# Third layer's time mixing (L2x): new x summed in the PSUM, copied out by ScalarE with sums and squares of the rows; VectorE's statistics for the last element only

## The reference, cut to what matters

```
x = x + tanh(g_xattn[2]) * wkv(time_decay, time_first, k=layernorm(x), v=ctx)
# wkv, per element and channel, w = -exp(time_decay), u = time_first:
#   y_t  = (e^(u+k_t) v_t + p_t) / (e^(u+k_t) + q_t)
#   p_t+1 = e^w p_t + e^(k_t) v_t ,  q_t+1 = e^w q_t + e^(k_t)      (computed with a running maximum)
x = x + tanh(g_ffn[2]) * experts(layernorm(x))       # needs mean and variance of each row of the new x
```

## Time and profile before

| | us |
|---|---|
| median of 3 runs (1809.58 to 1811.84) | 1811.55 |
| the profiled execution | 1814.82 |
| its span | 1813.1 |
| first and last VectorE instruction of L2x | 741.48 to 877.03 |

### The profile page before, as it was taken

One profiled execution on the slowest core, in us unless ns is written; L12 is line 12 of the kernel. 1 busy time (PEld: TensorE's weight loads), 2 busy tenths in 40 slices (PEclk: granted clock), 3 DMA queues, 4 the chain that ended last, 5 costly groups with the idle time before them and its releaser, 6 DMA issues. The chain is left out here.

```text
span 1813.1 us, 23758 instructions
## 1 busy us (share of the span) xinstructions
PE 1345.1 (74%) x6498; PEld 1003.8 (55%) x6518; DVE 1464.4 (81%) x3194; ACT 884.1 (49%) x1742; POOL 546.7 (30%) x560
## 2 busy tenths in 40 slices
PE   4799228886999677244662597179999899998788
PEld 2454114443788443243520486168888788877676
DVE  5999378984877568799579699796999889988785
ACT  3454356662333262353420242138888788843343
POOL 0000004543110021200004023303777577766552
PEclk8999759997999856566785799599999999999999
DMA  5010420000000120254100010405788799888874
GB/s 174 23 36 1 191 76 1 0 0 1 1 1 1 48 95 1 89 189 151 47 30 11 24 41 6 122 0 163 240 241 254 203 274 261 247 261 245 226 235 156
DMA packets 92284, 197.91 MB, mean 109 GB/s; under 512 B 16040, under 2 KB 25384, under 8 KB 91312
## 3 DMA queue, kind: packets, MB, share of 16 engines
q0 software_dynamic: 27120, 91.25, 18.0%
q1 hardware_dynamic: 65088, 105.82, 17.8%
HBM read 181.30 MB, written 15.73 MB: 109 GB/s over the span
## 5 line engine op out<-in xcount | busy, mean ns | idle before, releaser
L2246 POOL DMA_INDIRECT L3f_gd<-rows,idx x160 | 189.8, 1186 | 200.7 <-DVE L3f_gd L2475 176.1
L2246 POOL DMA_INDIRECT L3f_gu<-in_L_ffn_e_up,idx x160 | 168.9, 1056 | 71.3 <-issue 47.2
L2314 PE MATMUL L3f_o_ps<-L3f_euh,L3f_ath 128*128 128x512 f32 x352 | 146.0, 415 | 21.0 <-DVE L3f_atl L2456 20.9
L2302 PE MATMUL L3f_h_ps<-L3f_xh,L3f_edh 128*128 128x512 f32 (+1 forms) x384 | 145.1, 378 | 8.2 <-DVE L3f_xl L2461 8.2
L926 POOL TENSOR_TENSOR L0f_hq<-L0f_hid,magic 128x1408 bf16<-128x1408 f32 x16 | 45.2, 2826 | 338.9 <-DVE L0f_hid L997 338.9
L2302 PE MATMUL L3f_h_ps<-L3f_xh,L3f_edl 128*128 128x512 f32 (+1 forms) x384 | 144.5, 376 | 0.0
L2302 PE MATMUL L3f_h_ps<-L3f_xl,L3f_edh 128*128 128x512 f32 (+1 forms) x384 | 144.5, 376 | 0.0
L2286 PE MATMUL L3f_g_ps<-L3f_oh 128*128 128x128 f32 x704 | 97.6, 283 | 61.9 <-DVE L3f_oh L2443 61.9
L2314 PE MATMUL L3f_o_ps<-L3f_eul,L3f_ath 128*128 128x512 f32 x352 | 138.2, 393 | 0.0
L2314 PE MATMUL L3f_o_ps<-L3f_euh,L3f_atl 128*128 128x512 f32 x352 | 138.0, 392 | 0.0
L2286 PEld LDWEIGHTS L3f_g_ps<-L3f_oh 128*128 128x128 f32 x704 | 91.4, 195 | 72.5 <-issue 68.0
(11 more groups left out here) (529 smaller groups left out, 3669.5 us busy)
## 6 DMA issues: line engine op xcount, KB each, us to landing
L3f_eu<-in_L_ffn_e_up SPq DMA_DIRECT2D x96, 256.0 KB, 4.6
L3f_ed<-in_L_ffn_e_down SPq DMA_DIRECT2D x96, 256.0 KB, 4.4
L2x_ed<-in_L_ffn_e_down SPq DMA_DIRECT2D x32, 256.0 KB, 3.4
rows<-L2x_eo SPq DMA_DIRECT2D x32, 256.0 KB, 2.4
ternary_wgu<-in_L_ffn_w_gate_upT SPq DMA_DIRECT2D x4, 1408.0 KB, 10.3
X<-in_x SPq DMA_DIRECT2D x4, 1024.0 KB, 10.6
L0x_V<-in_ctxT SPq DMA_DIRECT2D x8, 512.0 KB, 3.4
L1f_C<-in_ctx SPq DMA_DIRECT2D x2, 2048.0 KB, 13.1
```

Of the source, the lines that this page charges most:

```text
L2246: pool.indirect_dma_start(buf[j % ND][:, :], None, table, bass.IndirectOffsetOnAxis(ap=idx[:, j:j + 1], axis=0)).then_inc(sem[j % ND], 16)
L2302: last = pe.matmul(h_ps[h][:, 0:cols], lhsT=w[h][:, c, :], rhs=x[:, c, 0:cols], start=(c == 0 and m == 0), stop=(c == DC - 1 and m == 2))
L2314: last = pe.matmul(o_ps[a][:, :], lhsT=w[h][:, a * P:(a + 1) * P], rhs=x[h][:, :], start=False, stop=False)
```

## The change

It applies to L2x alone (`own` is `not first`).

- `turn_back(b)`: the eight transposes become matmuls of y against `turner` (the identity times minus the tanh of the gate), added to what the PSUM holds. `begin_x(b)` puts X there first, by one f32 matmul 128x512 against the identity for each tile; it stands in TensorE's turn i behind the first two `turn_rows` and waits for the x of batch i-1 (`x_ready`).
- `add_to_x` is gone from VectorE. ScalarE's `keep_x(b)` copies the sum from the PSUM to X, with the sum of each row (`accum_out`), in turn b+1 between the first two `keep_rows` and `invert`. For the last element it copies without sums, and VectorE runs `bn_stats` on its two tiles.
- GpSimd makes the mean of each row from the sum (`mean_ready`); ScalarE's `deviate(b)` squares the distance to the mean, with its sum, at the end of turn b+1; the statistics of the next stage are filled in the form in which `bn_stats` leaves them (two equal halves' means, one sum of squares, one zero).
- VectorE computes `den` between the scans of q and p; before, it stood behind both.
- `turner` (128x128) is made by VectorE in place of `ntg` (128x1), ahead of the first statistics.

```diff
--- before.py
+++ after.py
@@ -167,6 +170,14 @@
     xn_ready, turned, ek_ready, ev_ready, q_ready, p_ready = (ph.sem(n) for n in ("xn", "turned", "ek", "ev", "q", "p"))
     den_ready, s_ready, p0_ready, ln_ready, r_ready = (ph.sem(n) for n in ("den", "s", "p0", "ln", "r"))
     t_ready, m_ready, y_ready, yT_ready, x_ready = (ph.sem(n) for n in ("t", "mr", "y", "yT", "x"))
+    own = not first
+    if own:
+        rowsum, part = ph.sb("rowsum", [P, NT]), ph.sb("part", [P, 1])
+        dev = [ph.sb(f"dev{j}", [P, D], BF16) for j in range(TB)]
+        part_made, mean_ready, dev_ready = ph.sem("part"), ph.sem("mean"), ph.sem("dev")
+    if not first:
+        turner = ph.sb("turner", [P, P])
+        turner_made = ph.sem("turner")
     if first:
         g = ph.sb("g", [P, 8])
         W, LT, tio = ph.sb("W", [P, DC, 2 * D]), ph.sb("LT", [P, DC, T]), ph.sb("tio", [P, T])
@@ -269,11 +280,22 @@
         def turn_back(b):
             pe.wait_ge(y_ready, b + 1)
             for j in range(TB):
+                if b and first:
+                    pe.wait_ge(x_ready, TB * (b - 1) + j + 1)
+                for c in range(DC):
+                    if first:
+                        last = pe.transpose(y_ps[j][:, c, :], y[:, c, j * P:(j + 1) * P], ident[:, :])
+                    else:
+                        last = pe.matmul(y_ps[j][:, c, :], lhsT=y[:, c, j * P:(j + 1) * P], rhs=turner[:, :],
+                                         start=False, stop=(c == DC - 1))
+                last.then_inc(yT_ready, 1)
+
+        def begin_x(b):
+            for j in range(TB):
                 if b:
                     pe.wait_ge(x_ready, TB * (b - 1) + j + 1)
-                for c in range(DC):
-                    last = pe.transpose(y_ps[j][:, c, :], y[:, c, j * P:(j + 1) * P], ident[:, :])
-                last.then_inc(yT_ready, 1)
+                pe.matmul(y_ps[j][:, :, :].rearrange("p c n -> p (c n)"), lhsT=ident[:, :], rhs=X[:, TB * b + j, :],
+                          start=True, stop=False)
 
         def project_k(b, j):
             if j == 0:
@@ -342,11 +364,16 @@
                 if i:
                     add_up(i - 1, 1)
             else:
+                if not i:
+                    pe.wait_ge(turner_made, 1)
                 if i:
                     turn_back(i - 1)
                 if i + 2 < B:
                     turn(i + 2)
-                for e in range(EU * i, EU * (i + 1)):
+                for e in range(EU * i, EU * i + 2):
+                    turn_rows(e)
+                begin_x(i)
+                for e in range(EU * i + 2, EU * (i + 1)):
                     turn_rows(e)
         if first:
             add_up(B - 1, 0)
@@ -404,6 +431,25 @@
             act.activation(r[:, :, :], den[:, :, :], ACT.Ln).then_inc(ln_ready, 1)
             act.wait_ge(ln_ready, b + 1)
             act.activation(r[:, :, :], r[:, :, :], ACT.Exp, scale=-1.0).then_inc(r_ready, 1)
+
+        def keep_x(b):
+            for j in range(TB):
+                t = TB * b + j
+                act.wait_ge(yT_ready, t + 1)
+                whole = y_ps[j][:, :, :].rearrange("p c n -> p (c n)")
+                if b < B - 1:
+                    act.activation(X[:, t, :], whole, ACT.Copy, accum_out=rowsum[:, t:t + 1]).then_inc(x_ready, 1)
+                else:
+                    act.activation(X[:, t, :], whole, ACT.Copy).then_inc(x_ready, 1)
+
+        def deviate(b):
+            act.wait_ge(mean_ready, b + 1)
+            for j in range(TB):
+                t = TB * b + j
+                if b:
+                    act.wait_ge(dev_ready, t + 1 - TB)
+                act.activation(dev[j][:, :], X[:, t, :], ACT.Square, scale=-1.0, bias=stats[:, t, 1:2],
+                               accum_out=stats[:, t, 2:3]).then_inc(dev_ready, 1)
 
         def keep_rows(e):
             k = e % 2
@@ -469,6 +515,8 @@
             if not first:
                 for e in range(EU * i, EU * i + 2):
                     keep_rows(e)
+                if i:
+                    keep_x(i - 1)
             invert(i)
             if i + 1 < B:
                 first_column(i + 1)
@@ -485,9 +533,15 @@
             else:
                 for e in range(EU * i + 2, EU * (i + 1)):
                     keep_rows(e)
+            if own and i:
+                deviate(i - 1)
         if first:
             for k in range(2):
                 keep(B - 1, k)
+        else:
+            keep_x(B - 1)
+        if own and first:
+            deviate(B - 1)
 
     @block.gpsimd
     def _(pool):
@@ -503,6 +557,14 @@
             for h in range(2):
                 for j in range(2):
                     pool.memset(sv[h][j][:, :, :, HD:HD + 1], 1.0).then_inc(filled, 1)
+        if own:
+            pool.memset(part[:, :], 1.0 / D).then_inc(part_made, 1)
+            pool.wait_ge(part_made, 1)
+            for b in range(B if first else B - 1):
+                pool.wait_ge(x_ready, TB * (b + 1))
+                ts = slice(TB * b, TB * (b + 1))
+                pool.tensor_tensor(stats[:, ts, 1:5:3], rowsum[:, ts].unsqueeze(2).to_broadcast([P, TB, 2]),
+                                   part[:, 0:1].unsqueeze(2).to_broadcast([P, TB, 2]), ALU.mult).then_inc(mean_ready, 1)
 
     @block.vector
     def _(dve):
@@ -526,6 +588,8 @@
             dve.scalar_tensor_tensor(rstd[:, sl], w1[:, sl], 1.5, rstd[:, sl], ALU.add, ALU.mult).then_inc(step, 1)
             dve.wait_ge(step, n + 3)
             dve.scalar_tensor_tensor(nm[:, sl], m[:, sl], -1.0, rstd[:, sl], ALU.mult, ALU.mult).then_inc(nm_ready, 1)
+            if own:
+                dve.memset(stats[:, sl, 5:6], 0.0)
             return n + 3
 
         def make_keys(b):
@@ -557,6 +621,13 @@
                 last = dve.tensor_tensor_scan(q[:, c, 1:T], a[:, c:c + 1].to_broadcast([P, T - 1]), ek[b % 2][:, c, 0:T - 1],
                                               0.0, ALU.mult, ALU.add)
             last.then_inc(q_ready, 1)
+            if not first:
+                dve.wait_ge(q_ready, b + 1)
+                if b:
+                    dve.wait_ge(y_ready, b)
+                for c in range(DC):
+                    last = dve.scalar_tensor_tensor(den[:, c, :], ek[b % 2][:, c, :], eu[:, c:c + 1], q[:, c, :], ALU.mult, ALU.add)
+                last.then_inc(den_ready, 1)
             dve.wait_ge(ev_ready, b + 1)
             if b:
                 dve.wait_ge(s_ready, b)
@@ -567,18 +638,14 @@
 
         def ratio(b):
             h = b % 2
-            dve.wait_ge(q_ready, b + 1)
-            if b:
-                dve.wait_ge(y_ready, b)
             if first:
+                dve.wait_ge(q_ready, b + 1)
+                if b:
+                    dve.wait_ge(y_ready, b)
                 dve.wait_ge(E_ready, b + 1)
                 dve.tensor_tensor(den[:, :, :], E[h][:, :, :], q[:, :, :], ALU.add).then_inc(den_ready, 1)
                 dve.wait_ge(den_ready, b + 1)
                 dve.tensor_tensor(E[h][:, :, :], E[h][:, :, :], V[b % 3][:, :, :], ALU.mult).then_inc(EV_ready, 1)
-            else:
-                for c in range(DC):
-                    last = dve.scalar_tensor_tensor(den[:, c, :], ek[h][:, c, :], eu[:, c:c + 1], q[:, c, :], ALU.mult, ALU.add)
-                last.then_inc(den_ready, 1)
             dve.wait_ge(p_ready, b + 1)
             dve.wait_ge(p0_ready, b + 1)
             if b:
@@ -645,8 +712,8 @@
             dve.wait_ge(made, 1)
             dve.tensor_scalar(kb[:, :], kb[:, :], -1.0, 19.0, ALU.mult, ALU.add).then_inc(u_ready, 1)
             dve.tensor_scalar(u[:, :], u[:, :], 83.0, None, ALU.min).then_inc(u_ready, 1)
-            dve.tensor_scalar(ntg[:, 0:1], tg[:, gate:gate + 1], -1.0, None, ALU.mult).then_inc(step, 1)
-            at = row_group(0, 1)
+            dve.tensor_scalar(turner[:, :], ident[:, :], tg[:, gate:gate + 1], -1.0, ALU.mult, ALU.mult).then_inc(turner_made, 1)
+            at = row_group(0, 0)
         if first:
             at = row_group(1, at)
             dve.wait_ge(gated, 1)
@@ -661,7 +728,7 @@
             if first:
                 context(i, 0)
             ratio(i)
-            if i:
+            if first and i:
                 add_to_x(i - 1)
             if first:
                 if 1 < i + 1 < NG:
@@ -670,7 +737,12 @@
             if i + 1 < B:
                 value(i + 1)
             invert(i)
-        add_to_x(B - 1)
+        if first:
+            add_to_x(B - 1)
+        else:
+            for t in range(NT - TB, NT):
+                dve.wait_ge(x_ready, t + 1)
+                dve.bn_stats(stats[:, t, :], X[:, t, :])
 
     ph.end()
 
```

## The result

The changed kernel takes 1801.8 us (median of 7 runs, 1800.05 to 1810.73) against 1811.84 for the kernel before, a ratio of 0.995 with a 95% interval of 0.9933 to 0.9966. The forecast was 1803.0.

What follows compares the result with a forecast made beforehand. VectorE bounds L2x until the squares' ring holds batches 2 to 5. Batch 0 +0.36, batch 1 -1.75, batches 2 to 5 -2.6, batch 6 -1.85, batch 7 -2.15, end -0.6, start +0.1: -8.5, from 1811.55 to 1803.0 us; range 1797 to 1809.

Steps and rivals of the forecast that it cites:

- VectorE is the bound, 2.51 off, 0.65 on: VectorE's batch in L2x: 15.05 us less 2.51 of x and statistics, plus 0.65 of exposed dependences, gives 13.2.
- The two dependences: On VectorE, den directly behind the scan of q and s behind the scan of p: 0.18 us each.
- the third: On VectorE, ev directly behind s: 0.29 us more per batch, already paid in batch 0.
- Copies and squares 1.6 and 1.8: ScalarE's additions per batch: two keep_x copies 1.6 us, two deviate squares 1.8 us, accumulator reads included.
- Batches 2 to 5 at 14.4, held by the squares' ring, -2.6: Ring through turn, keep_rows, row loads, deviate, weigh and normalise sets batches 2 to 5 at 14.4 us, saving 2.6 in all.
- the half microsecond that I granted it: TensorE's clock was expected to rise with begin_x, shortening the squares' ring from 14.9 to 14.4 us.
- The second ring, 13.3, little above VectorE: Ring from turn through keep_x, Ln and Exp, VectorE's L596 to L603 and turn_back: 13.3 us against VectorE's 13.2.
- `turn_back` costs nothing: On TensorE, eight f32 matmuls in place of eight transposes: 1.06 against 1.04 us, so no added time.
- the Trainium skill's rule of four: Rival 4: turn_back's matmuls cost four times the transposes, 6.9 us; second ring 18.5, total 1832 us; chance 0.03.
- Batch 7 -2.15, end -0.6: Last batch, without turn, weigh or normalise, gains 2.15 us; the end behind the last L603 shortens by 0.6.
- the table load: Rival 3: ScalarE's Square needs table loads, 1.28 us each, around each deviate; ring 17.0, total 1816 us; chance 0.07.
- VectorE alone: Rival 1: clock rises enough or rows land sooner, no ring above 13.2 us; total 1798.3 us; chance 0.22.

Runs made afterwards that it cites:

- the half of the change: Changed kernel with new x still copied out of the PSUM by ScalarE, but statistics left to VectorE's bn_stats; ratio 0.9975 to the kernel before, stage 116.29 us.
- the last kernel: Changed kernel with den behind both scans, squares behind normalise, last element's x as before, and zero-weight matmuls added; 1795.68 us against 1810.61 for the kernel before, ratio 0.9916.

## Why the prediction was right, and where it was not

The total was right (8.5 forecast; 8.9 in the stage, 10 in the median), and the bound engine was the right one. That it fits so closely is luck: batches 2 to 5 gave 3.15 us more than forecast, and the last batch and the end 1.34 and 1.80 less, 3.14 together.

- *VectorE is the bound, 2.51 off, 0.65 on* (right): 13.13 us measured against 13.2. The two dependences are 0.14 each in place of 0.18 (the kernel with den early, alone); the third is 0.29 as read from the earlier trace rows, and shows again in the half of the change.
- *Copies and squares 1.6 and 1.8* (too dear): 1.14 and 1.41. The accumulator read does not stand behind the instruction; it starts 0.13 us before its end, and the next starts 0.12 before the read's.
- *Batches 2 to 5 at 14.4, held by the squares' ring, -2.6* (the step that failed): they averaged 13.61 and gave 5.75. The ring is real and of the forecast size where the clock stays low (14.20 to 15.78 without the new matmuls), but the clock rose more than the half microsecond that I granted it: with TensorE at full clock the ring took 12.50 us, from `turn` at 784.65 to the end of `normalise` at 797.15, and bound nothing. Moving the squares out of the ring changed nothing; adding zeros to TensorE removed the waits.
- *The second ring, 13.3, little above VectorE* (the right path, mis-sized): this is the ring that made r late in batches 3 and 5, at 14.07 and 14.12. In batch 3 `turn_back` took 3.57 of it and not 1.7; the other four terms, 4.0, 1.6, 2.2 and 3.8, measured 3.41, 1.14, 2.19 and 3.76. With `turn_back` at full clock, in the kernel with zeros, it was no longer above VectorE's 13.13.
- *`turn_back` costs nothing* (wrong): it doubled, 2.05 us against 1.04 at full clock. The error is in reading: eight entries of L304 are four matmuls of the code, since each f32 matmul shows as two instructions, while a transpose is one. begin_x was mis-sized in the same way: 1.98 us at full clock, not 0.9. So TensorE got about 2 us more work a batch than the forecast counted; the granted clock with less and with more of such work (0.54, 0.64, 0.81, 0.91) points to it as the reason that the clock rose further.
- By the Trainium skill's rule of four ("TensorE: Matmul & The Clock Gate", Terms), `turn_back` would be 4 times as long; the trace shows 2 (2.05 against 1.04).
- By the Trainium skill, Part 4 of the same page, transposes do not engage the full clock. With transposes alone the stage was granted 0.54 to 0.59, and with matmuls in their place 0.64: the rule's direction holds here, but not the rule as it stands. In the kernel before TensorE does nothing but transposes from 814.02 to 818.47, and the clock rises to full while they run (`turn_rows` at 817.43 takes 1.04 us for eight). TensorE was also busier with the matmuls.
- *Batch 7 -2.15, end -0.6* (wrong, both for the same reason): -0.81 and +1.20. `turn_back` at half clock made r 1.30 late and the end longer; with the zeros they are 12.27 and 3.46 us. With `turn_back` by transposes and no begin_x batch 7 is 11.78, and the end, counted as in the forecast from the start of the last VectorE instruction on y, is 4.60 (1.22 and 3.38), against 11.85 and 4.6 forecast: the rest of those two sums was right.
- Rivals: the table load did not come. VectorE alone (1798.3) was nearer than its 0.22: four of six batches ran so.

Left open: behind the stage, from the first instruction of the next stage to the end of the span, the profiled executions took 935.7 us before, 941.2 after, and 933.1 in the last kernel. The differences lie mostly in L3f (659.2, 662.7 and 654.9 us from its first load), they do not follow the length of the stage, and no run was made to find their cause.

## What to carry to other kernels

When work moves off the engine that is the bound, write down what every other engine's queue needs for one turn, as a ring, and price the ring at both clock levels of TensorE: here the ring through the squares took 14.2 to 15.9 us without the new matmuls (stage clock 0.54) and 12.50 with TensorE at full clock, and the ring through `turn_back`, 14.07 with it at half clock, was no longer above 13.13 with it at full. Work given to an idle TensorE can shorten the path: before costing an f32 matmul, count the instructions of the row, not the calls of the code. And where the new order puts a reader right behind its writer, 0.14 to 0.29 us a time comes off the gain; leave one independent instruction between them.

## What the runs showed of the hardware

Two f32 matmuls 128x512 with zero weights per batch, 32 instructions in all, raised the granted clock of the stage from 0.81 to 0.91, though the result is unchanged, and gave a stage of 108.8 us where two profiles without them had 113.4 and 116.9. An f32 matmul 128x128 is two instructions of about 0.13 us at full clock and 0.24 at half (2.05 and 3.78 us for 16), an f32 transpose one (1.04 us for eight at full clock). GpSimd's product of four numbers per row took 0.26 to 1.19 us in the changed kernel; it was never waited for.
